# Third layer norm of a Mamba and cross-attention kernel: sums of channel halves on GpSimd, squares on ScalarE

## The reference, cut to what matters

```
xn = layernorm(x, ln1);  yn = layernorm(context, ln2)
q  = xn @ Wq;  k, v = yn @ Wkv          # 16 heads of 16
o  = softmax(q k^T / 4) v
x  = x + (o @ Wproj + bproj)
h  = gelu(layernorm(x, ln3) @ W1 + b1)  # 256 -> 1024
x  = x + (h @ W2 + b2)

layernorm: mu = mean(x); var = mean((x - mu)^2); (x - mu) * rsqrt(var + 1e-5) * w + b
```

## Time and profile before

| what | value |
|---|---|
| median of three runs | 7791.65 us |
| the profiled execution: time | 7799.68 us |
| the profiled execution: span | 7797.9 us |
| mean granted TensorE clock | 0.985 |
| the norm stage, last block, first mean to first up job | 22.3 us |

### The profile page before, as it was taken

The page is one execution under the profiler, slowest core; times in us unless marked ns, Lnnn a source line. Parts: engine busy times, 40 slices in busy tenths (PEclk is TensorE's granted clock), DMA queues, the critical chain, the costliest instruction groups (busy, mean ns, idle before and its releaser), DMA issues. The chain is left out here.

```text
span 7797.9 us, 204883 instructions
## 1 busy us (share of the span) xinstructions
PE 7253.6 (93%) x86656; PEld 5168.7 (66%) x86656; DVE 6486.4 (83%) x6490; ACT 5772.7 (74%) x10871; POOL 5816.9 (75%) x2981
## 2 busy tenths in 40 slices
PE   7998799999988999999988999999989999999989
PEld 4666577777764677777764677777764677777765
DVE  5999799999984699999973699999973799999972
ACT  5777788888864688888864788888854788888853
POOL 4994599899970599999970598899960689899960
PEclk9999999999999999999999999999999999999999
DMA  3323222223210222222210222222210222222210
GB/s 104 90 82 94 69 75 70 75 75 97 76 47 23 82 75 70 78 86 89 70 52 21 78 75 70 87 88 77 71 52 22 78 75 74 97 80 73 70 52 11
DMA packets 736041, 552.24 MB, mean 71 GB/s; under 512 B 355844, under 2 KB 679364, under 8 KB 698008
## 3 DMA queue, kind: packets, MB, share of 16 engines
q1 hardware_dynamic: 735128, 539.13, 22.2%
HBM read 519.25 MB, written 19.79 MB: 69 GB/s over the span
## 5 line engine op out<-in xcount | busy, mean ns | idle before, releaser
L1229 DVE TENSOR_TENSOR_SCAN arena<-arena,ps 128x512 f32<-128x512 f32 x4608 | 5291.7, 1202 | 389.8 <-issue 254.1
L1454 POOL TENSOR_TENSOR arena<-arena 128x1024 f32<-128x1024 f32 x2240 | 5248.0, 2367 | 489.7 <-DVE arena L1229 461.3
L904 ACT ACTIVATE arena<-arena,rate 128x511 f32<-128x511 f32 (+1 forms) x4608 | 3033.5, 709 | 11.6 <-DVE arena L1229 11.2
L569 PEld LDWEIGHTS ps<-arena 64*128 64x128 f32 x36864 | 2322.4, 189 | 1073.1 <-issue 614.8
L569 PE MATMUL ps<-arena 64*128 64x128 f32 x36864 | 2712.8, 285 | 184.1 <-DVE arena L1229 175.3
L588 PE MATMUL ps<-csts,arena 64*128 64x64 f32 x35840 | 1519.3, 223 | 8.3 <-POOL arena L1454 8.0
L588 PEld LDWEIGHTS ps<-csts,arena 64*128 64x128 f32 x35840 | 1436.3, 139 | 18.4 <-POOL arena L1454 12.3
L627 PE MATMUL ps<-arena 128*128 128x512 f32 x1152 | 594.5, 632 | 164.6 <-DVE arena L1259 154.3
L1474 POOL TENSOR_TENSOR arena<-arena 128x512 f32<-128x512 f32 x288 | 371.2, 1289 | 410.6 <-PE ps L654 242.5
L668 PE MATMUL ps<-arena 128*128 128x512 f32 x1120 | 588.6, 631 | 3.1 <-DVE hT L1269 3.1
L632 PE MATMUL ps<-arena 128*128 128x512 f32 x1120 | 567.0, 621 | 3.7 <-DVE arena L1259 2.3
(11 more groups left out here) (116 smaller groups left out, 6454.1 us busy)
## 6 DMA issues: line engine op xcount, KB each, us to landing
arena<-c_rows SPq DMA_DIRECT2D x288, 1024.0 KB, 5.2
arena<-b_image SPq DMA_DIRECT2D x576, 256.0 KB, 3.2
arena<-ip_x SPq DMA_DIRECT2D x20, 512.0 KB, 4.4
arena<-ip_z SPq DMA_DIRECT2D x20, 512.0 KB, 4.5
arena<-op_w SPq DMA_DIRECT2D x20, 512.0 KB, 6.7
hT<-xT SPq DMA_DIRECT2D x16, 512.0 KB, 3.8
arena<-w SPq DMA_DIRECT2D x8, 1024.0 KB, 5.2
out<-arena SPq DMA_DIRECT2D x64, 128.0 KB, 1.7
```

Source lines behind the costliest of these rows:

```text
L569: i = nc.tensor.matmul(o, dtxT[half[h], c, b, :], diagB[half[h], pair, b, :].rearrange("p (i s) -> p i s", s=Q), start=True, stop=True)
L904: nc.scalar.activation(o, i, ACT.Exp, scale=rate[:, ph.layer(n), g:g + 1]).then_inc(decay.sem, 1)
L1229: nc.vector.tensor_tensor_scan(hs[:, place(n, v) + g % 2, :], dA[:, g % RING, :], pair[:, g % Q::Q], 1.0 if ph.main() else 0.0, ALU.mult, ...
L1454: nc.gpsimd.tensor_tensor(hs[:, a:a + 2, :], hs[:, a:a + 2, :], Crep[:, 2 * pair:2 * pair + 2, :], ALU.mult).then_inc(prod.sem, 1)
```

## The change

The mean of the third norm is made from one matmul call: GpSimd first adds the two channel halves of X[b] into sq[:, b, 0], and TensorE multiplies that sum with `ones_x`. The variance is made in the same way: ScalarE squares the centred halves (in place of VectorE), GpSimd adds the two halves of the squares, TensorE makes one call. GpSimd's eight new additions stand behind its eight oT multiplies. The orders of the four engines in this stage are now four lists; TensorE's order of jobs is the one of before.

```diff
+NORM_PE = [("mean", 0), ("proj", 2), ("mean", 1), ("var", 0), ("proj", 3), ("mean", 2), ("var", 1), ("mean", 3),
+           ("var", 2), ("var", 3)]
+NORM_DVE = [("residual", 0), ("residual", 1), ("centre", 0), ("residual", 2), ("centre", 1), ("residual", 3), ("centre", 2),
+            ("scale", 0), ("centre", 3), ("scale", 1), ("scale", 2), ("scale", 3)]
+NORM_ACT = [("square", 0), ("square", 1), ("root", 0), ("square", 2), ("root", 1), ("shift", 0), ("square", 3), ("root", 2),
+            ("shift", 1), ("root", 3), ("shift", 2), ("shift", 3)]
+NORM_POOL = [("sum", 0), ("sum", 1), ("squares", 0), ("sum", 2), ("squares", 1), ("sum", 3), ("squares", 2), ("squares", 3)]
...
                 def mean3(b):
-                    product(bk, ("mean3", b), [(ones_x, X[b][k]) for k in range(KD)], read=[("proj", b, k) for k in range(KD)])
+                    pe.wait_ge(apl.sem, apl.upto(bk, f"sum{b}"))
+                    product(bk, ("mean3", b), [(ones_x, sq[:, b, 0, :])])
 
                 def var3(b):
-                    pe.wait_ge(av.sem, av.upto(bk, f"dsq{b}"))
-                    product(bk, ("var3", b), [(ones_x, sq[:, b, k, :]) for k in range(KD)])
...
+                    pe.wait_ge(apl.sem, apl.upto(bk, f"squares{b}"))
+                    product(bk, ("var3", b), [(ones_x, sq[:, b, 0, :])])
...
-                root(bk, ("var3", 0), rs[:, 0, :])
-                root(bk, ("var3", 1), rs[:, 1, :])
-                shifted(0, yna, ln3_b, "yn")
...
+                def squared(b):
+                    act.wait_ge(av.sem, av.upto(bk, f"den{b}"))
+                    await_read(act, bk, ("mean3", b))
+                    nc.scalar.activation(sq[:, b, :, :], yna[:, b, :, :], ACT.Square).then_inc(asc.sem, 1)
...
                     for k in range(KD):
                         i = nc.vector.tensor_tensor(out[:, b, k, :], X[b][k], abank((job, b)), ALU.subtract)
                         i.then_inc(av.sem if k == 0 else read_sem((job, b)), 1)
+                    if job == "mean3":
+                        return
...
                     nc.gpsimd.tensor_tensor(oT[:, b, m, :], oT[:, b, m, :], rden[:, u % 2, :], ALU.mult
                                             ).then_inc(apl.sem, 1)
+                for what, b in NORM_POOL:
+                    if what == "sum":
+                        for k in range(KD):
+                            await_read(pool, bk, ("proj", b, k))
+                        one, two = hT[:, b, 0, :], hT[:, b, 1, :]
+                    else:
+                        pool.wait_ge(asc.sem, asc.upto(bk, f"dsq{b}"))
+                        one, two = sq[:, b, 0, :], sq[:, b, 1, :]
+                    nc.gpsimd.tensor_tensor(sq[:, b, 0, :], one, two, ALU.add).then_inc(apl.sem, 1)
```

More of the change, by code:

```diff
@@ L417, in program @@
         loop_ends = len(jobs)
-        last = [("mean3", 0), ("proj", 2, 0), ("proj", 2, 1),
-                ("mean3", 1), ("var3", 0), ("proj", 3, 0), ("proj", 3, 1), ("mean3", 2), ("var3", 1), ("mean3", 3),
-                ("var3", 2), ("var3", 3)]
+        last = []
+        for what, b in NORM_PE:
+            last += [("proj", b, m) for m in range(KD)] if what == "proj" else [(what + "3", b)]
         eight = len(jobs) + len(last)
@@ L481, in program @@
         av = Steps(sem("attention_vector"), vector_order
-                   + ["den0", "dsq0", "den1", "dsq1", "den2", "dsq2", "yn00", "yn01", "den3", "dsq3"]
-                   + [f"yn{b}{k}" for b in (1, 2, 3) for k in range(KD)])
+                   + [name for what, b in NORM_DVE
+                      for name in {"centre": [f"den{b}"], "scale": [f"yn{b}0", f"yn{b}1"]}.get(what, [])])
         scalar_order = []
@@ L490, in program @@
                     ["crs", "cb0", "cb1", "cb0d", "cb1d", "sq3", "rs3"] + scalar_order
-                    + ["r30", "r31", "yb00", "yb01", "r32", "yb10", "yb11", "r33", "yb20", "yb21", "yb30", "yb31"])
+                    + [name for what, b in NORM_ACT
+                       for name in {"square": [f"dsq{b}"], "root": [f"r3{b}"], "shift": [f"yb{b}0", f"yb{b}1"]}[what]])
         fore = Steps(sem("first_norms"), ["sq0", "ln0", "rs0", "sd0", "lv0", "rv0", "sq1", "xa0", "xb0", "ln1", "rs1", "sd1",
                                           "lv1", "rv1", "xa1", "xb1", "sq2", "ln2", "rs2", "sd2", "lv2", "rv2", "xa2", "xb2"])
-        apl = Steps(sem("attention_pool"), [f"kbd{b}{m}" for b, m in units] + [f"o{b}{m}" for b, m in units])
+        apl = Steps(sem("attention_pool"), [f"kbd{b}{m}" for b, m in units] + [f"o{b}{m}" for b, m in units]
+                    + [f"{what}{b}" for what, b in NORM_POOL])
         stored = [sem("stored0"), sem("stored1")]
@@ L812, in mean3 @@
                 def mean3(b):
-                    product(bk, ("mean3", b), [(ones_x, X[b][k]) for k in range(KD)], read=[("proj", b, k) for k in range(KD)])
+                    pe.wait_ge(apl.sem, apl.upto(bk, f"sum{b}"))
+                    product(bk, ("mean3", b), [(ones_x, sq[:, b, 0, :])])
                 def var3(b):
-                    pe.wait_ge(av.sem, av.upto(bk, f"dsq{b}"))
-                    product(bk, ("var3", b), [(ones_x, sq[:, b, k, :]) for k in range(KD)])
[L819 to L828, removed]
+                    pe.wait_ge(apl.sem, apl.upto(bk, f"squares{b}"))
+                    product(bk, ("var3", b), [(ones_x, sq[:, b, 0, :])])
+                for what, b in NORM_PE:
+                    {"proj": proj, "mean": mean3, "var": var3}[what](b)
                 def down(b, r):
@@ L1184, in attend @@
                         turned(2 * (x - TURN_LAG) + 1)
-                root(bk, ("var3", 0), rs[:, 0, :])
-                root(bk, ("var3", 1), rs[:, 1, :])
-                shifted(0, yna, ln3_b, "yn")
[L1188 to L1192, removed]
+                def squared(b):
+                    act.wait_ge(av.sem, av.upto(bk, f"den{b}"))
+                    await_read(act, bk, ("mean3", b))
+                    nc.scalar.activation(sq[:, b, :, :], yna[:, b, :, :], ACT.Square).then_inc(asc.sem, 1)
+                for what, b in NORM_ACT:
+                    if what == "square":
+                        squared(b)
+                    elif what == "root":
+                        root(bk, ("var3", b), rs[:, b, :])
+                    else:
+                        shifted(b, yna, ln3_b, "yn")
                 for j in MLP_ORDER:
@@ L1363, in scaled @@
                 def scaled(b, x, w, rname, squares):
-                    done(f"{squares}{b}")
+                    if squares:
+                        done(f"{squares}{b}")
                     dve.wait_ge(asc.sem, asc.upto(bk, f"{rname}{b}"))
@@ L1401, in residual @@
                                                        ALU.add, ALU.add).then_inc(read_sem(j), 1)
[L1403 to L1413, removed]
+                for what, b in NORM_DVE:
+                    if what == "residual":
+                        residual(b)
+                    elif what == "centre":
+                        centre("mean3", b, "den", yna)
+                    else:
+                        scaled(b, yna, ln3_w, "r3", None)
                 dve.wait_ge(aw_loaded, bk * 48 + 48)
```

## The result

The changed kernel took 7823.65 us (median of 5, 7819.32 to 7830.87) against 7794.12 us of the kernel before: ratio 1.0039, 95% interval 1.0026 to 1.0051. Measured once more beside 23 runs of before it took 7818.74 against 7796.07, ratio 1.0030 (1.0019 to 1.0041). That is 23 to 30 us slower, where 13 were forecast; the range ended at 7813. Of the distance between 7804.7 and 7823.65, 2.5 us are the base: the forecast stands on the median of three runs of before, 7791.65, and that of five is 7794.12.

A forecast was written before the change was run, and what follows sets the result against it. PE's chain through the norm stage to the first up job bounds the kernel. Waits of 0.65 us plus two clock drops of 1.3 give 3.25 us per block, 13 in all, on 7791.65: 7805 us, range 7793 to 7813.

The forecast's parts named there:

- PE's start of the first up job: End of the norm stage: the instant PE starts the first up job decides; 22.27 us per block before.
- the wait behind o31: Before mean3(0): GpSimd's early sums stand behind its last multiply, leaving PE idle 4.15 us.
- the second to fourth gaps: PE waits for GpSimd additions before mean3(3), var3(2) and var3(3): 0.8, 1.65 and 2.55 us.
- Both drops: PE at half clock over mean3(0) and proj(2), again over var3(3) and first up jobs: 1.3 us each per block.
- the sum of 3.75 us: Per-block cost if both clock drops come in every block: 0.65 + 1.4 + 1.7 us, 15 in all.
- The full-clock term: Norm stage without clock drops: 22.9 us against 22.27, so +0.65 us per block.
- The step that failed: Norm-stage delay passes one for one in the last block, moves MLP and next block elsewhere: 3.25 us per block, 13 total.
- the step reading: From the follow-up runs' forecasts: small delays change block periods by whole 3.4 us steps or not at all.
- A: Norm stage: no clock drop, or one only; 7794 at full clock, 7799.5 with the first alone; chance 22%.
- D: Norm stage: squares on ScalarE bring table loads; some 7815 us; chance 2%.
- C: Norm stage faster: PE's own work bounds it, gaps two to four close, 4.3 us less per block, 7774; chance 5%.
- B: Norm stage: GpSimd additions bound it and take over 1.45 us; 5.25 us per block, +21, 7813; chance 13%.

The follow-up runs named there:

- e2: Changed kernel with PE's idle time before mean3(0), var3(2) and var3(3) filled by four, one and two useless matmul calls; 7812.29 us, ratio 1.0019.
- g2: Kernel before plus two extra matmul calls (1.72 us) ahead of mean3(0) in every block; ratio 1.0036, +28.9 us.
- e3: Changed kernel keeping only the squares on ScalarE: no GpSimd additions, two matmul calls each for mean and variance; 7809.23 us, ratio 1.0017.
- g1: Kernel before plus one extra matmul call (0.86 us) ahead of mean3(0) in every block; ratio 1.0013, +10.8 us.
- g4: Kernel before plus four extra matmul calls (3.44 us) ahead of mean3(0) in every block; ratio 1.0018, +14.0 us.
- h1: Kernel before plus two extra matmul calls (1.72 us) ahead of mean3(0) in the first block alone; 7807.77 us, ratio 1.0009.
- e6: e4 plus two useless matmul calls (1.72 us) ahead of mean3(3); 7777.24 us, ratio 0.9970 to the kernel before.
- e4: e1 with scale 0 and shift 0 made earlier and up(0,0), up(0,1) worked before var3(2), var3(3); 7786.34 us, ratio 0.9985 to before.
- e5: e4 with scale 0 behind centre 2 and square 2 ahead of shift 0, keeping scale 0 off sum(3); 7785.68 us, ratio 0.9982.
- e1: Changed kernel with GpSimd's sum(0) and sum(1) moved ahead of its last multiply o31; 7802.22 us, ratio 1.0006 to the kernel before.

## Why the prediction was wrong, point by point

**Right:** that PE's start of the first up job decides the stage; the wait behind o31 (4.15 forecast, 4.00 measured); the second to fourth gaps (0.8, 1.65, 2.55 against 0.55, 1.35, 2.18); additions at 1.27, squares at 1.06 without table loads; the removed calls turned into waiting (at full clock +0.65 forecast, +0.4 in e2); low clock over mean3(0) and proj(2) and over var3(3) and the first up jobs. The stage was forecast at +3.25 us and measured at +3.5 in six of eight blocks. Both drops came in all eight, as in the sum of 3.75 us that the prediction set beside the Trainium skill. But that section ("TensorE: Matmul & The Clock Gate", "HAM oscillation") describes waits of 3 to 5 us, which is the first gap's size alone; none of the three gaps ahead of the second drop is over 2.2 us.

**Mis-sized:** the terms for the two drops. I priced each as one low stretch of 3.4 us, at 1.3 us. Where each is one stretch they cost 3.1 us together, 1.55 each. In blocks 3 and 4 of the first profile both drops lasted 6.8 us, and the stage cost 6.4. The full-clock term was too large by 0.25 us.

**The step that failed** is the first paragraph's "A delay there reaches the end one for one in the last block. In the other three it moves the MLP, and the next block's first steps with it", and the sum's "3.25 us per block, 13 us for four" that rests on it. In the last block it holds (93.06 us of MLP in every profile). In the others the block is no rigid body. In the changed kernel's second profile the four stages cost 14.0 us, close to the 13 forecast, and the run is 22.6 us longer: 8.6 us came from stretches that the sum has at nothing. The medians of other kernels say the same: g2's 1.72 us per block cost 28.9 in all and e3's -0.6 cost +13, and neither interval holds the linear price (g1's 0.86 cost 10.8 and g4's 3.44 cost 14.0). I had looked at what waits for PE, and not at which of the block's other gaps sit at the edge of a clock drop. In the profile of before PE has eight gaps of 2 to 4.1 us per period, and a shift of one or two microseconds decides for several of them whether 3 to 10 us run at 1.2 or at 2.4 GHz.

**Where the rest of the time is.** The granted clock of the 13 traces places it. The MLP of blocks 1 to 3 is the same work in every kernel, and its length goes by the low clock in it (39 cases, each within 0.1 us of its row):

| low clock in the MLP, us | 0 | 3.4 | 6.8 | 10.2 | 13.7 |
|---|---|---|---|---|---|
| length of the MLP, us | 133.3 | 135.0 | 136.0 | 137.1 | 138.3 |
| cases | 5 | 22 | 5 | 6 | 1 |

For the whole run take what lies between the end of the first block's attention products and the end of the program, without the four norm stages. Against the profile of before:

| kernel | low clock there, us | time there, us |
|---|---|---|
| g4 | -13.6 | -3.4 |
| changed, again | +16.9 | +6.4 |
| g1 | +32.1 | +11.0 |
| e3 | +40.1 | +15.2 |
| h1 | +44.4 | +15.4 |
| g2 | +53.4 | +18.8 |

A line of 0.34 us for each microsecond at the low clock meets all 13 profiles within 1.2 us. So what an edit cost or gave outside the stage is how much more or less of the unchanged work ran at 1.2 GHz.

**What the steps are.** All 39 periods of 13 profiles lie within 0.35 us of 1744.2 plus or minus whole multiples of 3.4 us, as long as the shortest low stretch in the rows. This much is measured. A reading that fits: work that resumes inside a low stretch gains back half of any delay (it then has less of its time at half speed), and behind the seven to twelve low stretches of a period little is left of an odd shift. That is an argument from rows 10 to 12 and the periods; no run here took the low stretches out of the whole block, so it is not shown. Which step a kernel lands on I can't derive: the step reading missed g2, h1 and e6.

**Rivals.** A (no second drop) is out by the timelines, and D since no table load stands beside the 16 new squares. C's sign came by its letter (the gaps sum to 8.1 us, under its 8.5), but not at full clock: with e2's +0.4 us they come to some 8.9 there (an estimate, 22.27 + 0.4 - 13.8), and the stage was longer and not shorter. B ended on the right side for a wrong reason: additions take 1.27 us in the changed kernel. e4 and e5 agree with the exclusion rule that stood beside it, but it costs nothing in the changed kernel, where scale instructions keep to 747 ns in the mean and 753 at most.

## What to carry to other kernels

Moving work to another engine also moves it behind that engine's queue: ask for each new wait what stands ahead of it in program order, and put what is ready early ahead of what comes late (e1: 5.8 us of the stage for two moved additions). Removed TensorE work is worth something only once the order lets later jobs fill the holes (e4 and e6: 37 us of stage against 43). Where TensorE's clock drops several times per iteration, compare segments of the timeline and not totals: below some 0.4% here the total tells where gaps fell, and two useless matmuls per block cost four times their length in one kernel (g2) and came with a shorter time in another (e6).

## What the runs showed of the hardware that I had not expected

The same gap of 2.03 us is followed by half speed or not, depending on where it falls (3.19, 1.98, 3.41 us for one job in three kernels). A low stretch after one gap lasts 3.4 us or 6.8 with PE about equally busy in it (2.86 and 2.80 of 3.40 us). An MLP of unchanged work takes 133.3 to 138.3 us by how much of it runs at the low clock. A VectorE pair with both operands in SBUF takes 2.42 us beside a GpSimd addition and 1.41 without. And the kernel before alone spreads over 19 us in 83 runs (7787.85 to 7807.24), more than most edits here moved it.
